# Four transformer layers in one pipeline: TensorE's order around the maxima, the last attend and the output projection

## The reference

```
L0  h = gamma * rmsnorm(x) + beta
    q, k, v = h Wq^T, h Wk^T, h Wv^T          # 16 heads of 16
    x = x + alpha * (softmax(q k^T / 4) v) Wo^T
    h = gamma' * rmsnorm(x) + beta'
    x = x + alpha' * ((silu(h Wg^T) * (h Wh^T)) Wout^T + b)
L1  h = rmsnorm(x) * scale;  val, gate = split(h Wup^T)
    x = x + quant(val * gelu(gate)) ternary(Wdown)^T
L2  x = x + relu(x (Wd + dWd)^T + bd) (Wu + dWu)^T + bu   # dWd, dWu made from the condition
L3  out = (layernorm(x) * w + b + tanh(...)) * w + b
```

## Time and profile before

| | |
|---|---|
| median of three runs | 1133.96 us (1133.51 to 1135.20) |
| the profiled execution | 1136.88 us, of which its trace spans 1135.1 us |
| TensorE busy | 1004.5 us, 88%, 7362 matmuls, mean granted clock 0.961 |
| VectorE busy | 791.6 us, 70% |
| ScalarE busy | 535.0 us, 47% |
| GpSimd busy | 197.4 us, 17% |
| one batch in the loop | 62.1 us (`attend(a, 3)` starts at 346.81 and again at 408.92) |

### The profile page before, as it was taken

The page is one execution under the profiler, slowest core; times in us unless marked ns, Lnnn a source line. Parts: engine busy times, 40 slices in busy tenths (PEclk is TensorE's granted clock), DMA queues, the critical chain, the costliest instruction groups (busy, mean ns, idle before and its releaser), DMA issues.

```text
span 1135.1 us, 22223 instructions
## 1 busy us (share of the span) xinstructions
PE 1004.5 (88%) x7362; PEld 848.2 (75%) x7362; DVE 791.6 (70%) x1755; ACT 535.0 (47%) x1100; POOL 197.4 (17%) x235
## 2 busy tenths in 40 slices
PE   5269779999999999999999999999999999997964
PEld 4124659797887879796978888797969798886852
DVE  3644467777777788787777777777877777776552
ACT  2245264545545463646454454636364545545320
POOL 2351101111121212021111212120202111121210
PEclk9679899999999999999999999999999999999985
DMA  9888203040403112130404030211304040300000
GB/s 333 272 301 288 84 17 107 1 132 2 127 5 104 27 63 67 38 93 1 130 1 130 1 114 16 76 54 38 92 1 130 1 130 1 121 2 19 2 19 9
DMA packets 78049, 89.45 MB, mean 79 GB/s; under 512 B 18672, under 2 KB 64640, under 8 KB 75392
## 3 DMA queue, kind: packets, MB, share of 16 engines
q1 hardware_dynamic: 71792, 62.81, 18.4%
q0 software_dynamic: 2304, 16.78, 4.1%
q10 hardware_dynamic: 3920, 9.44, 2.2%
HBM read 63.14 MB, written 25.31 MB: 78 GB/s over the span
## 4 chain that ended last, share of the span: by engine, by line
PE 67%; DVE 14%; ACT 6%; DMA 5%; issue 4%; SPq 3%; POOL 1%; DVEq 0%; ACTq 0%; POOLq 0%
PE bank L552 16%; PE bank L589 14%; PE bank L564 7%; PE bank L513 7%; PE bank L458 5%; PE bank L497 5%; PE bank L523 4%; PE bank L531 3%; DMA k_dram<-probs 2%; ACT h L764 2%; PE bank L627 1%; DMA w_raw<-w_upT 1%; PE bank L600 1%; PE bank L621 1%; DVE den_x L1080 1%
## 5 line engine op out<-in xcount | busy, mean ns | idle before, releaser
L1049 DVE TENSOR_REDUCE neg_max<-bank 128x2 f32<-128x512 f32 x256 | 165.1, 684 | 35.5 <-PE bank L497 35.5
L425 POOL TENSOR_TENSOR act_lo<-act_f,act_hi 128x256 fp32r<-128x256 f32 x128 | 94.4, 738 | 427.4 <-ACT act_hi L846 427.4
L811 ACT ACTIVATE probs<-bank 128x512 f32<-128x512 f32 x256 | 138.5, 592 | 36.0 <-PE bank L513 34.0
L840 ACT ACTIVATE silu_g<-bank 128x256 f32<-128x256 f32 x128 | 49.1, 384 | 201.7 <-PE bank L552 201.5
L497 PE MATMUL bank<-k_stack,q_stack 128*128 128x512 f32 x256 | 85.6, 417 | 31.4 <-DMA k_stack<-k_dram 30.7
L513 PE MATMUL bank<-q_stack,k_stack 128*128 128x256 f32 x512 | 107.4, 326 | 6.5 <-DMA q_stack<-few_rows 2.7
L513 PEld LDWEIGHTS bank<-q_stack,k_stack 128*128 128x128 f32 x512 | 75.6, 190 | 46.3 <-ACT probs L811 32.3
L589 PE MATMUL bank<-up_hi,h_hi 128*128 128x256 f32 x512 | 106.7, 290 | 1.6 <-DVE act_u L1152 0.6
L552 PE MATMUL bank<-h_hi,gh_hi 128*128 128x256 f32 x512 | 103.4, 283 | 3.6 <-DVE h_lo L1110 3.6
L552 PE MATMUL bank<-h_lo,gh_hi 128*128 128x256 f32 x512 | 103.7, 284 | 0.0
L552 PE MATMUL bank<-h_hi,gh_lo 128*128 128x256 f32 x512 | 102.8, 282 | 0.0
(11 more groups left out here) (150 smaller groups left out, 2160.2 us busy)
## 6 DMA issues: line engine op xcount, KB each, us to landing
hyper<-w_hyper POOLq DMA_DIRECT2D x16, 1024.0 KB, 7.8
q_stack<-q_dram SPq DMA_DIRECT2D x96, 128.0 KB
k_stack<-k_dram SPq DMA_DIRECT2D x96, 128.0 KB
q_dram<-probs SPq DMA_DIRECT2D x16, 512.0 KB, 2.8
k_dram<-probs SPq DMA_DIRECT2D x16, 512.0 KB, 3.6
delta_dram<-hyper_s ACTq DMA_DIRECT2D x16, 256.0 KB, 5.7
x_res<-xT SPq DMA_DIRECT2D x16, 256.0 KB, 2.9
out<-xc SPq DMA_DIRECT2D x16, 256.0 KB, 2.5
```

The costliest lines, as they stand in the source:

```text
L425: pool.tensor_tensor(act_lo[:, c % 3, :], act_f[:, c % 2, :], act_hi[:, c % 3, :].bitcast(F32), ALU.subtract).then_inc(g_lo.sem, 1)
L811: act.activation(probs[:, h % SLOTS], halves(h % 2), ACT.Exp, scale=float(H / D) ** 0.5).then_inc(s_exp.sem, 1)
L1049: dve.tensor_reduce(neg_max[:, qt, :, pair:pair + 1].rearrange("p a o -> p (a o)"), halves(n % 3), AX_X, ALU.max, negate=True).then_inc(ma ...
```

## The change

TensorE's queue alone is changed. In turn 8 of the first stretch `ffn_out(f, 6)` goes first, then `norm_a(nxt)`, then `max_turn(a)`; before, it was `max_turn`, `norm_a`, `ffn_out`. In the second stretch `project_v(nxt, 0)` goes ahead of `attend(a, 3)`, with its wait for VectorE's fifth step of the same batch's normalisation now written there and a wait for the finished `h1` (`n1_dve`) beside it. In the third stretch `project_v(nxt, 1)` goes behind `ln_mean(g)`, ahead of `project(a)`.

```diff
--- before.py
+++ after.py
@@ -474,8 +474,6 @@
                         mm.then_inc(done.sem, 1)
 
                 def project_v(b, t):
-                    if t == 0 and b.follows():
-                        pe.wait_ge(o_dve.sem, o_dve.at(b, 5, back=1))
                     for c in range(DC):
                         mm = pe.matmul(halves(2)[:, t, :], h1[:, c, t * P:(t + 1) * P], w_qkv[:, c, 2 * D:3 * D],
                                        start=(c == 0), stop=(c == DC - 1))
@@ -665,16 +663,16 @@
                         if a and c < FC:
                             max_scores(a, 2 * c)
                             max_scores(a, 2 * c + 1)
+                        if f and c >= 2:
+                            ffn_out(f, c - 2)
+                        if nxt and c == FC:
+                            if f:
+                                pe.wait_ge(g_dve.sem, g_dve.at(f, 7))
+                            norm_a(nxt)
                         if a and c == FC:
                             if starts(a):
                                 pe.wait_ge(small_in.sem, 16 * 6)
                             max_turn(a)
-                        if nxt and c == FC:
-                            if f:
-                                pe.wait_ge(g_dve.sem, g_dve.at(f, 7))
-                            norm_a(nxt)
-                        if f and c >= 2:
-                            ffn_out(f, c - 2)
                         if starts(a) and c in (1, 3, 5, 7):
                             hyper_product(4 + c // 2)
                     if starts(a):
@@ -701,6 +699,10 @@
                                 scores(a, 4 * t + 5)
                             if t == 2 and f:
                                 pe.wait_ge(x2_dve.sem, x2_dve.at(f, DC))
+                            if t == 3 and nxt:
+                                pe.wait_ge(n1_dve.sem, n1_dve.at(nxt))
+                                pe.wait_ge(o_dve.sem, o_dve.at(a, 5))
+                                project_v(nxt, 0)
                             attend(a, t)
                             if t < 3:
                                 scores(a, 4 * t + 6)
@@ -712,6 +714,8 @@
                         project_qk(nxt)
                     if g:
                         ln_mean(g)
+                    if nxt:
+                        project_v(nxt, 1)
                     if starts(a):
                         hyper_product(13)
                     if a:
@@ -720,14 +724,10 @@
                         project(a)
                     if g:
                         ln_var(g)
-                    if nxt:
-                        project_v(nxt, 0)
                     if starts(a):
                         hyper_product(14)
                     if a:
                         norm_f(a)
-                    if nxt:
-                        project_v(nxt, 1)
                     if starts(a):
                         hyper_product(15)
                     if f:
```

## The result

The changed kernel takes 1150.95 us in the median (four runs, 1150.05 to 1155.3) against 1134.15 for the kernel before (1133.51 to 1135.2). The ratio is 1.0162, with a 95% interval from 1.0136 to 1.0188. The forecast was 1148.4 us, in a range from 1139 to 1154. So it is slower by 16.8 us in the medians, where 14.4 were expected.

A forecast was written before the change was run, and what follows sets the result against it. TensorE's in-order queue was taken as the bound. Thirteen regular batches at 0.8 + 0.13 (12.1 us), plus 0.5, 0.55 and 1.3 for batches 1, 15 and 0, gave 14.4 us on 1133.96: 1148.4 us, range 1139 to 1154.

The forecast's parts named there:

- The way from `max_turn` to `scores(0)`: Copy of the maxima and two DMAs: 3.64 us that no TensorE work shortens, making `scores(0)` 1.19 us late.
- `ffn_out(6)` waits for POOL: Ahead of `max_turn`: it needs POOL's low part of chunk 6, fills only 0.36 us; `max_turn` comes 1.28 us later.
- `norm_g`'s wait absorbs 0.41: Behind `scores(0)` in a steady batch: 0.41 us of the 1.19 us delay is absorbed, since `norm_g` waited there anyway.
- VectorE's lag costs nothing: Behind `mlp_down(g, 1)`: VectorE comes 1.2 us later, TensorE 0.8; the 0.4 between them was expected to add no stop.
- the term of +0.8: Regular batches, `ffn_out(6)` and `norm_a` ahead of `max_turn`: +0.8 us a batch, bounds +0.65 and +1.1.
- Part B: Value projection halves moved ahead of the last `attend` and `project`: stops only move, +0.1 us a batch, +0.13 in the sum.
- part A: `ffn_out(6)` and `norm_a` ahead of `max_turn`: the DMA of the maxima is no longer hidden, +0.8 us a batch.
- Batch 0: First batch, without FFN: `max_turn` falls in behind `norm_a`, which waits for the square; +1.3 us, bounds 0 and 1.8.
- Batches 1 and 15: No `mlp_down` in batch 1, no next `norm_a` in batch 15: little absorbs the later `max_turn`; +0.5 and +0.55 us.
- The early DMA (1): Before `scores(0)`: the maxima's DMA lands early and `mlp_down` alone binds, so 0.36 us a batch is gained; 1131 us, 6%.
- The gain of part B (2): Behind `norm_f`: filled stops are real gains because `up` takes in what TensorE saves, 0.7 us a batch; 1138 us, 10%.
- The clock (3): Longer stops drop TensorE's clock, a price of 1.2 us each time; 1164 us, 5%.

The follow-up runs named there:

- Part A alone: Against the kernel before, only `ffn_out(6)` and `norm_a` put ahead of `max_turn`, value projection as before: 1150.21 us, ratio 1.0168.
- e2: Against the kernel before, only both halves of the value projection moved, order around the maxima as before: 1132.74 us, ratio 1.0001.

## Why the prediction held, point by point

- **The way from `max_turn` to `scores(0)` can't be covered any more: right, and a little larger.** 3.64 us were put and 3.73 measured. The 3.73 stand in the earlier trace rows too, as 395.15 - 391.42; I read the steady batch as bound by `mlp_down` and took the shorter figure of batch 15. The stop before `scores(0)` is 1.78 us, just outside the 1.2 to 1.6 that were named.
- **`ffn_out(6)` waits for POOL: right.** It starts 0.05 us behind POOL, with a stop of 0.42. `max_turn` comes 2.38 us after the last matmul of `ffn_out(5)` (394.67 in the same timeline) against 1.06 before (390.36): 1.32 later, where 1.28 was put.
- **`norm_g`'s wait absorbs 0.41: right.** It comes 1.46 us behind `scores(0)` instead of 1.88.
- **VectorE's lag costs nothing: wrong by 0.08.** From `norm_g` to the last `attend` it takes 414.21 - 402.24 = 11.97 us instead of 408.92 - 397.03 = 11.89. The delay shows at `adapter_down`: it starts 0.80 us behind the scores ahead of it instead of 0.69, and its row is 1.10 us long instead of 1.03. That is 0.18, of which `norm_g`, now without a stop, gives 0.10 back. The sum of the terms as measured is 1.32 - 0.42 + 0.08 = 0.98, against a batch that is 0.98 longer. Part A alone is 1.02, so the term of +0.8 was mis-sized by 0.2.
- **Part B is neutral: right.** +0.13 was put and +0.05 measured. `project` starts 6.28 us behind `attend(3)` instead of 6.13, but without a stop in front its matmuls (four in the code, eight in the profile's count) reach `ln_var` after 1.73 instead of 1.83 (422.22 in the same timeline, for `project`; 416.88 before), and that pays most of it back. `norm_f` to the fourth chunk kept its 6.2 us. All the stops that were named ahead are there, with 0.93 for the one before `norm_f` where 1.1 was named. On top of part A it is -0.04 (63.06 against 63.11). That 0.93 was put for a batch and 0.98 measured is luck in part: part A was put 0.2 too low and part B 0.1 to 0.2 too high.
- **Batch 0: the term that was most off.** +1.3 was put with a bound of 1.8, and 3 to 4 measured. The sum took 3.64 us for the way of the maxima; in batch 0 it takes 84.11 - 78.66 = 5.45 us, 4.78 of them from ScalarE's copy to `scores(0)`, against 400.78 - 397.47 = 3.31 in a regular batch. Weights and the hypernetwork's matrices are still being loaded then: the DMA engines are busy 0.83 of the time in those 4.78 us, and 0.02 of it from 397 to 401. That the loads slow the two small DMAs fits this but was not tried by itself.
- **Batches 1 and 15: +0.5 and +0.55 were put, less measured.** From the `project` of the batch ahead to that of batch 15 it takes 61.82 us instead of 61.48 (+0.3). For batch 1 it takes 60.50 instead of 61.16 (-0.7): the loss that was put is not there. Part A alone has 60.60, and why is open.
- **The sum.** Counted between the `project` of one batch and the next, in the two profiled executions: -0.7 for batch 1, 13.2 for batches 2 to 14 (of which batch 2 alone, 62.72 instead of 61.40, makes 1.3), 0.3 for batch 15. With 3.8 for batch 0 (the difference of the means above) that makes 16.6 of the 16.8 us. The total thus came near the forecast by errors that partly cancel: about 2.5 too little for batch 0 and 1.1 for the regular batches, 1.4 too much for batches 1 and 15.
- **Rivals.** The early DMA (1) is excluded by nine stops of 1.78 us. The gain of part B (2) is excluded by e2 at +0.05 us a batch, where the rival had -0.7. The clock (3) stayed at its full level, 2.4 GHz, through the loop: it is granted at 1.00 over 300 to 900 us, and moving 0.89 us of work into the stop gave all of it back.

## What to carry to other kernels

A stop before an instruction is worth filling only with work that is ready by then and fits; `norm_a` did, while `ffn_out` waited for POOL and delayed a transpose from which it is 3.7 us, over a copy and two DMAs, to the matmul that needs its result. Look at what hides the way behind the instruction before putting anything ahead of it: here the steady batch hid it to a tenth of a microsecond, and only batches 1 and 15 showed it bare. Where two stops lie on either side of a chain through other engines, filling the first opens the second, and the gain comes from shortening the chain (a VectorE step moved behind another, one line) with the filled stops on top.

## What the runs showed of the hardware

Whole executions of one kernel differ by up to 8 us here (23 executions of the kernel before took from 1128.39 to 1136.33), while its regular batches repeat to 0.15. Two differences stand in the traces, one at the start and one at the end. ScalarE's square in batch 0 starts at 78.69 in the kernel before and at 76.13 in the changed one, and anywhere from 72.71 to 78.69 in the twelve traces, though nothing that ScalarE does ahead of it was changed; just ahead of it ScalarE waits for a DMA of the weights (2.40 us in the kernel before). And the last 20 us, in which TensorE works in short bursts, are granted different clocks. The windows of the kernel before and of e2 over the same last work (stretch; length, busy time of PE, PEld, DVE, ACT, POOL; granted clock; DMA share; GB/s):

```profile
1112.28:1132.28 20.00, 10.22 (x24) 5.71 (x22) 4.97 (x11) 1.52 (x3) 2.31 (x4) 0.50 0.00 0
```

```profile
1106.43:1125.40 18.97, 6.34 (x26) 3.64 (x24) 4.97 (x11) 1.52 (x3) 2.52 (x4) 0.77 0.04 14
```

At 0.50, the lower level of 1.2 GHz, TensorE is busy 10.22 us, and at 0.77, part of it at the full level, 6.34. (The kernel before runs 2.82 us past its window, without a matmul.) Behind batch 15's `max_turn` the kernel before needs 122.8 us to the end and e2 119.0, though no instruction there is ordered otherwise: the edit moves projections that batch 15 doesn't have. The 3.9 us between them lie in these windows. What made the clock differ is open. A change of 0.1 or 0.2 us a batch is therefore read from the length of a batch, not from the medians.
